# Self-attention to past states: the first negated maxima turned in another bank and earlier, with a lead of nine steps

## What is computed

```python
scores = einsum('bhsd,bhtd->bhst', q, k) * SCALE
output = merge_heads(einsum('bhst,bhtd->bhsd', softmax(scores), v)) @ Wo + bo
rq = split_heads(output @ Wrq + brq)
rk, rv = split_heads(past @ Wrk + brk), split_heads(past @ Wrv + brv)
rattn = softmax(einsum('bhsd,pbhtd->pbhst', rq, rk) * SCALE)
recursive = merge_heads(einsum('pbhst,pbhtd->pbhsd', rattn, rv)).mean(axis=0)
gate = sigmoid(concat([output, recursive]) @ Wg + bg)
x = layernorm(x + output * (1 - gate) + recursive * gate)
```

## Time and profile before

| | |
|---|---|
| median of 3 runs | 627.39 us (626.36 to 627.66) |
| the profiled execution's own time | 628.19 us |
| its span | 626.4 us |
| instructions | 14025 |
| granted PE clock, mean of the span | 0.95 |
| PE busy | 529.5 us |
| VectorE busy | 454.5 us |
| ScalarE busy | 332.5 us |

### The profile page before, as it was taken

How to read it: one execution, slowest core, us unless ns; L and a number is a source line. 1 busy time by engine, 2 the same in 40 slices (tenths; PEclk the granted TensorE clock), 3 DMA queues, 4 the chain that set the end, 5 groups by cost and what they waited for, 6 DMA issues and landing times.

```text
span 626.4 us, 14025 instructions
## 1 busy us (share of the span) xinstructions
PE 529.5 (85%) x5226; PEld 288.9 (46%) x5226; DVE 454.5 (73%) x1017; ACT 332.5 (53%) x572; POOL 215.0 (34%) x333
## 2 busy tenths in 40 slices
PE   2587878699999999999988887778999987989884
PEld 0254454223333333333334555543443466878773
DVE  4466656778899898998945577837667757958586
ACT  2165646358778778777766466550111163427761
POOL 6113211701111331331231415062344274766342
PEclk9889989779999999999999799998999997979798
DMA  5448541030001101021002123044755600001001
GB/s 152 108 120 231 140 119 50 2 102 2 2 2 53 29 25 52 2 54 52 2 2 70 40 66 103 3 136 138 257 172 178 222 0 2 2 17 35 2 18 50
DMA packets 44542, 44.04 MB, mean 70 GB/s; under 512 B 6902, under 2 KB 35318, under 8 KB 44342
## 3 DMA queue, kind: packets, MB, share of 16 engines
q1 hardware_dynamic: 42460, 42.01, 23.0%
q10 hardware_dynamic: 2016, 1.15, 0.7%
HBM read 25.18 MB, written 1.18 MB: 42 GB/s over the span
## 4 chain that ended last, share of the span: by engine, by line
PE 58%; DVE 12%; ACT 9%; issue 8%; DMA 7%; POOL 4%; ACTq 1%; SPq 1%; DVEq 0%; POOLq 0%
PE banks L1159 12%; PE banks L1139 7%; PE banks L1078 5%; PE banks L552 5%; PE banks L1752 4%; PE banks L462 4%; ACT probs L699 4%; PE banks L535 3%; DMA past_mem<-gates 2%; DMA shared<-neg_T 2%; PE banks L1170 2%; DVE rec_negmax L1388 1%; DVE left L412 1%; DVE shared L1866 1%; PE banks L1118 1%
## 5 line engine op out<-in xcount | busy, mean ns | idle before, releaser
L1388 DVE TENSOR_REDUCE rec_negmax<-banks 128x2 bf16<-128x512 f32 x256 | 165.7, 688 | 25.9 <-PE banks L1078 21.2
L1281 ACT ACTIVATE probs<-banks 128x1024 f32<-128x1024 f32 x128 | 130.9, 1024 | 52.0 <-PE banks L1139 51.1
L843 DVE TENSOR_REDUCE negmax<-banks 128x8 bf16<-128x1024 f32 x64 | 78.2, 1222 | 53.7 <-PE banks L510 53.7
L1078 PE MATMUL banks<-shared 62*128 62x512 bf16 x256 | 97.8, 401 | 4.2 <-DVE rec_negmax L1388 3.9
L1139 PE MATMUL banks<-shared 64*128 64x256 bf16 x512 | 97.3, 279 | 1.4 <-DMA shared<-rec_neg_T 1.4
L1159 PE MATMUL banks<-probs,past_mem 128*32 128x256 f32 x1024 | 83.2, 397 | 1.3 <-ACT o_T L1288 1.3
L699 ACT ACTIVATE probs<-banks 128x1024 f32<-128x1024 f32 x64 | 65.4, 1022 | 32.3 <-PE banks L535 32.1
L1752 PE MATMUL banks<-shared,w_r 128*128 128x512 f32 x128 | 61.2, 617 | 5.0 <-DVE shared L1866 5.0
L1139 PEld LDWEIGHTS banks<-shared 64*128 64x128 bf16 x512 | 29.9, 94 | 72.1 <-issue 65.6
L552 PE MATMUL banks<-probs,shared 128*32 128x128 f32 x1024 | 43.1, 288 | 14.6 <-ACT probs L699 14.4
L1866 DVE TENSOR_TENSOR shared<-past_mem,out_T 128x512 f32<-128x512 f32 x64 | 42.9, 694 | 15.2 <-DMA past_mem<-gates 14.1
(11 more groups left out here) (248 smaller groups left out, 983.3 us busy)
## 6 DMA issues: line engine op xcount, KB each, us to landing
past_mem<-gates SPq DMA_DIRECT2D x64, 256.0 KB, 5.1
shared<-qk_parts SPq DMA_DIRECT2D x90, 128.0 KB, 2.5
shared<-past_mem SPq DMA_DIRECT2D x30, 128.0 KB, 2.4
xk_T<-in_x_T SPq DMA_DIRECT2D x4, 256.0 KB, 3.3
w_r<-in_w_r SPq DMA_DIRECT2D x1, 1024.0 KB, 6.1
shared<-rec_neg_T SPq DMA_DIRECT2D x64, 2.0 KB
xk_T<-in_ctx_T SPq DMA_DIRECT2D x4, 256.0 KB, 3.4
past_mem<-in_ctx_T SPq DMA_DIRECT2D x8, 128.0 KB, 2.2
```

The source lines that it names most:

```text
L843: nc.vector.tensor_reduce(c.negmax[:, i % 2, :].rearrange("p (r j) -> p r j", r=2)[:, :, 4 * half:4 * half + 4], c.max_pair.rearrange("p ( ...
L1078: self.nc.tensor.matmul(c.max_banks[r], c.QT[64 * r:64 * r + 62, g % 2, j, off:off + P], c.rKT[64 * r:64 * r + 62, j, :], start=True, stop ...
L1281: nc.scalar.activation(c.probs[:, i % 4, :], c.score_pairs[i % 2], ACT.Exp, scale=HEAD_SCALE)\
L1388: self.nc.vector.tensor_reduce(out, c.max_banks[r].rearrange("p (a t) -> p a t", a=NP_PAST), AX_X, ALU.max, negate=True).then_inc(s["rec_m ...
```

## The change

The first turn of maxima moves to bank 7, where it needs no claim on `misc` but waits until ScalarE has copied the last maxima of self-attention (`self_neg`, 16) and the norm of item 13 (`self_ctx_t`, 14) out of that bank. It is issued at the beginning of slot 17, behind its first lead. The next turn of a norm into that bank (item 14) waits for ScalarE's copy of the maxima. That copy stands before the last exponential. `LEAD` is 9, and slot 16 has a seventh early step (place 4, on PE before the projection, on VectorE before place 2). The tail of self-attention moves: context turn from step 0 to 4, normalisation from 1 to 5, norm turn and its copy from 4 to 6.

```diff
 def turn_norm(i):                                # PE, attention
+    if not cross and i == B - 2:
+        pe.wait_ge(*s.after("rec_neg", 1))
     nc.tensor.transpose(norm_out(c, ph, i), ...)
 def slot(t):                                     # PE
     ...
     elif lead:
         lead(t, 0)
+    if lead and t == SELF_SLOTS - 1:
+        lead(t, 3)
     ...
     if 0 <= t - 3 < B:
         turn_norm(t - 3)
-    if lead and t == SELF_SLOTS - 1:
-        lead(t, 3)
+    if lead and t == B:
+        lead(t, 4)
     if t < B:
         project_v(t)
     window(t)
 def slot(t):                                     # ACT
     ...
     if t:
         window(t - 1)
+    if tail:
+        tail(t, 3)
     if 0 <= t - 2 < B:
         exp(t - 2, 1)
     if 0 <= t - 3 < B:
         copy_norm(t - 3)
-    if tail:
-        tail(t, 2)
 def slot(t):                                     # DVE
     ...
+    if lead and t == B:
+        lead(t, 4)
     if lead and t >= B:
         lead(t, 2)
-LEAD = 10
+LEAD = 9
+def past_neg(c, n, q):
+    bank = c.banks[:, 7, P:2 * P] if (n, q) == (0, 0) else c.banks[:, 0, 0:P]
+    return bank.bitcast(BF16)[0:8, :]
 def self_tail(self, own, k):                     # PE
-    if k == 0:
+    if k == 4:
         self.claim("self_norm", B)
         own.turn_ctx(B - 1)
-    if k == 4:
+    if k == 6:
         self.claim("self_ctx_t", B)
         own.turn_norm(B - 1)
 def turn_max(self, n, q):
     pe.wait_ge(*s.after("rec_max", 2 * (STEPS * n + 4 * q + 4)))
-    self.claim("rec_neg", 4 * n + q + 1)
+    if (n, q) == (0, 0):
+        pe.wait_ge(*s.after("self_neg", B))
+        pe.wait_ge(*s.after("self_ctx_t", B - 2))
+    else:
+        self.claim("rec_neg", 4 * n + q + 1)
     for v in range(2):
-        last = self.nc.tensor.transpose(c.misc.bitcast(BF16)[0:8, v * P:(v + 1) * P], ...)
+        last = self.nc.tensor.transpose(past_neg(c, n, q)[:, v * P:(v + 1) * P], ...)
 def copy_neg(n, q):                              # ACT
-    nc.scalar.copy(c.rec_neg_T[:, q, :], c.misc.bitcast(BF16)[0:8, 0:PAIR]).then_inc(s["rec_neg"], 1)
+    nc.scalar.copy(c.rec_neg_T[:, q, :], past_neg(c, n, q)).then_inc(s["rec_neg"], 1)
 def in_self(t, place):
-    if (t, place) == (SELF_SLOTS - 1, 2):
+    if (t, place) == (SELF_SLOTS - 1, 3):
         copy_neg(0, 0)
 def self_tail(own, k):                           # ACT
-    if k == 4:
+    if k == 6:
         own.copy_norm(B - 1)
 def self_tail(self, own, k):                     # DVE
-    if k == 1:
+    if k == 5:
         own.normalise(B - 1)
```

More of the change, by code:

```diff
@@ L1115, in turn_max @@
         pe.wait_ge(*s.after("rec_max", 2 * (STEPS * n + 4 * q + 4)))
-        self.claim("rec_neg", 4 * n + q + 1)
+        if (n, q) == (0, 0):
[3 more added lines that the diff above has]
+            self.claim("rec_neg", 4 * n + q + 1)
         for v in range(2):
-            last = self.nc.tensor.transpose(c.misc.bitcast(BF16)[0:8, v * P:(v + 1) * P], c.rec_negmax[:, n % 2, q, v, :],
+            last = self.nc.tensor.transpose(past_neg(c, n, q)[:, v * P:(v + 1) * P], c.rec_negmax[:, n % 2, q, v, :],
                                             c.ident_b[:, :])
```

## The result

The changed kernel takes 622.28 us (median of 4 runs, 620.07 to 624.60), the kernel before 627.52 us beside it (626.36 to 629.92). The ratio is 0.9889 with a 95% interval of 0.9845 to 0.9933: 5.2 us less, and 622.28 us where 622.4 us was forecast. The profiled execution took 624.20 us, its span is 622.4 us. Every ratio in this text is formed from the executions in the faster of the chip's two states, and need not be the quotient of the two medians.

What follows compares the result with a forecast made beforehand. It took PE, the matmul engine, as the bound, with its waits and clock. A 5.5 us gain at step 5's exponential, less 0.2, 0.1 and 0.2, gave 5.0 off the 627.39 us median: 622.4 us, range 619.4 to 625.9.

Steps and rivals of the forecast that it cites:

- The late projection: Slot 16: the added early step makes the projection wait on VectorE's reductions and start 1.27 us late.
- The turn and the copy sooner: Ahead of the last self-attention exponential: first maxima turned at 112.2 instead of 112.82, copied 0.97 us sooner.
- First past scores: Start of past attention: the 1.44 us DMA wait goes, late PE work replaces it, start only 0.2 us sooner.
- The double steps and the wait behind them: Past steps 0 to 3: steps 0 and 1 end unchanged, 1.37 us wait goes, two double steps fewer save 2.92 us.
- The clock: Self-to-past attention: clock still falls to half, rises between 125 and 130, taken as 127.3; gain at step 5's exponential 5.5 us.
- the third set of rows: Transfers queued on SyncE behind nine others: some 8 us available until step 8, nothing counted, bounds 0 and -1.56 us.
- The norm turn in step 6 and the claim behind it: Past steps 6 and 7: norm turn at full clock costs 0.2 us, the later bank claim 0.1 us.
- The end of the stage: End of past attention: last pair of maximum products moves one step later, to step 6, costing 0.2 us.
- A: Clock stays at half until step 5's scores: net gain 3.3 us, 624.1 us; chance 0.25 together with D.
- D: First maxima's turn waits on the fifth pair, nothing sent ahead, 1.44 us DMA wait stays; within A, joint chance 0.25.
- B: Clock never falls between self and past attention: step 5's exponential at 126.5, net gain 7.85 us, 619.5 us; chance 0.10.
- C: Later half-clock stretches give the gain back: 625.8 to 627.5 us, or 629.2 us; chance 0.12 no change, 0.05 slower.

Runs made afterwards that it cites:

- e4: Kernel before with the early turn of the first maxima alone; seam (slot 16's first past maximum products to step 5's exponential) 30.96 us, total 629.78 us, ratio 1.003.
- e1: Kernel before with the self-attention tail alone moved (context turn to step 4, normalisation 5, norm turn 6); seam 29.19 us, total 627.05 us, ratio 1.000.
- e3: Kernel before with LEAD = 9 and the moved tail, first maxima still turned late; seam 26.91 us, total 623.36 us, ratio 0.994.
- e11: Changed kernel without the seventh early step; seam 27.43 us, total 623.84 us, ratio 0.994 to the kernel before.
- e10: Changed kernel with the first maxima's turn back in the shared bank and its copy behind the last exponential; seam 26.16 us, total 623.14 us, ratio 0.993.
- e6: Changed kernel with nine added matrix products, their result overwritten, in steps 0 and 1; seam 23.24 us, total 623.53 us, ratio 0.993.
- e7: Changed kernel with the third and fourth set of maxima rows issued first on SyncE; seam 24.34 us, total 621.66 us, ratio 0.993.
- e9: Changed kernel run again, nothing altered; seam 24.42 us, total 622.85 us, ratio 0.993 to the kernel before.
- e8: Changed kernel with both the third and fourth rows issued first and the nine added products; seam 23.24 us, total 621.21 us, ratio 0.990.
- e2: Kernel before with LEAD = 9 alone; seam 28.42 us, total 628.26 us, ratio 1.001.

## Why the prediction was right, point by point

- **The late projection.** Forecast 1.27 us; it starts 110.50 - 106.33 = 4.17 us behind the first pair, before 107.38 - 104.58 = 2.80: 1.37. Right: the wait on VectorE's reductions stands there as named, in two parts (0.53 and 0.21).
- **The turn and the copy sooner.** Forecast 0.97 us for the copy; measured from the first pair 8.94 before and 8.20 after, so 0.74. The turn waited for the fifth pair, as the working had it, and came 0.27 later than I put it.
- **First past scores.** Forecast 0.2 us sooner; 11.54 before, 117.69 - 106.33 = 11.36 after: 0.18. As forecast, the transfer wait went and late PE work took its place (0.64 us for the last exponential). Without the seventh step, in e4, the scores did start 0.70 us sooner, and steps 0 and 1 ate it up.
- **The double steps and the wait behind them.** I took steps 0 and 1 to end where they had; the second turn then came 1.37 us sooner. Measured 18.44 and 17.42, so 1.02: the end of steps 0 and 1 came 0.35 us later than taken, with VectorE's ten reductions back to back. The lost double steps and the clock are read together: from the second turn to step 5's exponential 11.83 before, 6.90 after, 4.93 less where the working had 5.5 - 1.37 = 4.1.
- **The clock.** It fell, as expected, also with the gap filled (PE's longest wait ahead of it 0.68 us). Forecast back at 127.3 in the positions of before; in those it came back at 126.6 - 1.75 = 124.9, at the very edge of the 125 to 130 I gave and 2.4 sooner than the value I took. With that, and the 0.35 us lost ahead of it, the seam became 24.32 us and not 24.77. Here luck had a part. I took the 4.3 us between PE's last wait on VectorE and the rise from a single example. It was 4.2 before and 4.0 in the changed kernel, but 5.0 in e1, 5.5 in e3, 6.3 in e11 and 7.0 in e10. Three us more at half clock would have taken up to 1.5 us off the gain (an estimate, from half the length).
- **Behind the seam.** Here a term failed: "so I count nothing, bounded by 0 and -1.56" for the third set of rows. PE waits for it 0.75 us in the changed kernel, 1.59 in e6, and not at all in e7. The mistake was to give the set its whole time from turn to step 8. That time was 133.93 - 127.47 = 6.5 us and not 8, and the SyncE queue was busy until 131.4 with nine transfers that had themselves started only when the second set was out. The earlier the seam ends, the more this wait grows: none in e10 (26.16 us), 0.66 in e9 (24.42), 1.59 in e6 (23.24). The norm turn in step 6 and the claim behind it I had at 0.3; from the exponential of step 5 to that of step 8 it takes 4.57 us in e7 and 4.09 before, so 0.48. The end of the stage I had at 0.2; from step 8 to the last exponential it is 192.46 us after and 192.41 before, so 0.05.
- **Sum.** Forecast 5.5 at the seam and 5.0 at the end; measured 5.95, then 4.61 over the stage, 5.2 in the medians of four and some 4.4 by e9's ratio. Two errors of size met: the gain at the seam was 0.45 above the forecast, the loss behind it 1.34 and not 0.5. That they nearly cancel, and that the medians of four agree with the forecast within 0.2 us, is luck; the mechanism and the order of the terms are what was right.

Of the rivals, A (clock down to step 5) did not come, nor D: PE no longer waits on the first rows. B's price was off: I gave it an exponential of step 5 at 126.5, or 21.9 us behind the first pair, and e6, with no fall, has 23.24. Most of the 1.3 us lies in steps 0 and 1: B has the second turn 16.5 us behind the first pair, e6 17.44, of which 0.32 is the added product ahead of it. B counted eight reductions from 116.1, and VectorE has ten in a row there. The Trainium skill, page "TensorE: Matmul & The Clock Gate", section "HAM oscillation", lays such falls at idle gaps between bursts of matrix products; the waits on a DMA in its example are longer than any gap here. In this trace, filling the one of 1.44 us did not keep the clock up in the changed kernel, whose longest wait ahead of the fall was 0.68 us. Its advice, to keep PE at work, agrees with e6 and e8: with added products no fall came in the seam. C, the later stretches, is real as scatter and not as a trend: see below.

## What to carry to other kernels

Where an engine waits for one that reduces its results, a piece moved ahead pays only if its inputs are ready by then: the early turn alone cost 0.7 us at the seam; on the changed kernel, with one more step of work ahead of it, it gave 1.8. Work that merely catches up (a longer lead than its consumer needs) is cheapest left undone: one step less of it gave 1.85 us alone, more than the moved tail (1.1) or the early turn did alone, and 2.9 on the changed kernel. And after shortening a stretch, look at the queue of transfers that nobody had to wait for so far.

## What was unexpected

The same instructions ahead of the seam took 103.27 us in the profiled execution of e11 and 108.16 us in that of e2, though both kernels have them alike up to slot 16. The granted clock tells why: e11 has none of the half clock of e2 (20 us stretches of PE, first two lines e2, last two e11, from its own table):

```profile
0.00:20.00 20.00, 4.39 (x12) 0.81 0.64 167
20.00:40.00 20.00, 16.22 (x185) 0.59 0.41 105
```

```profile
0.00:20.00 20.00, 4.39 (x12) 1.00 0.63 167
20.00:40.00 20.00, 14.93 (x189) 1.00 0.39 106
```

Behind past attention it is similar: from the last exponential to the end of the span it took between 290.3 us (e3) and 295.8 us (e4), again with more and fewer stretches at half clock. Each of the two parts thus scatters by some 5 us, with such stretches that lie elsewhere from execution to execution; that is enough to hide parts of 1 to 2 us in a total. What decides where the stretches fall was not tried.
